# Ternary stage's weights, magnitudes, threshold, first ternary part and first two rows moved into the rotated attention's last batch

## The chip, the cores and the metric

One core of one Trainium2 chip. The metric is the device time of one execution in microseconds, the median of several runs. TensorE multiplies, VectorE, ScalarE and GpSimd compute elementwise and by rows, SyncE issues the transfers.

## The reference

A sequence of four layers, each an attention and a feed-forward part, all added to the residual x of 2048 rows by 512 (four sequences of 512). The change touches layer 2:

```python
x = x + _L2_attn_ref(_layernorm(x, axis=-1), q_w, q_b, kv_w, kv_b, o_w)
x = x + _L2_ffn_ref(_layernorm(x, axis=-1), w_fc, w_proj)

def _L2_attn_ref(x, q_w, q_b, kv_w, kv_b, o_w):
...
    q = _rope((x @ q_w.T + q_b) * scale)
    k = _rope(k)
    attn = jax.nn.softmax(jnp.einsum('bse,bte->bst', q, k), axis=-1)
    return jnp.einsum('bst,bte->bse', attn, v) @ o_w.T

def ternarize_weights(w):
    gamma = jnp.mean(jnp.abs(w))
    return jnp.sign(jnp.round(w / (gamma + EPS))) * gamma
def bitlinear(x, w):
    xn = layer_norm(x)
    x_hat = xn + jax.lax.stop_gradient(absmax_quant(xn) - xn)
    w_hat = w + jax.lax.stop_gradient(ternarize_weights(w) - w)
    return jnp.einsum('bsd,od->bso', x_hat, w_hat)
```

`_L2_ffn_ref` is bitlinear with w_fc, gelu, bitlinear with w_proj. A ternary weight can only be made once the mean magnitude of its whole matrix (w_fc or w_proj, 4 MB each) is known.

## The kernel before, in words

P = 128 partitions, D = 512, DC = 4 chunks of D, NB = 4 batches of TT = 4 tiles of 128 rows, NT = 16 tiles ("rows" below: row 0 is tile 0). The residual x stays in SBUF as 16 tiles. `build` calls one function for each stage; each stage is one `nc.Block`, in which every engine has its own program, and the next block starts when all engines have ended this one. Within a block the engines wait for one another by semaphores. An engine executes in order: whatever stands behind a waiting instruction waits too. `Jobs` gives each use of one of the eight PSUM banks a number, from which the waits for a bank being full, read or vacant follow. `product` (L99 to L103) makes one product out of three matmuls on high and low parts (fp32r pairs); `pair` reserves the high and low parts.

**attention512** ("a2", L1341). `ORDER` (L1390) is the order of the jobs by hand, and all five engines but SyncE walk through it. A batch is: four turns of the normalised rows ("T"), eight projections of q and k ("qk"), four of U = x times the folded value and output weights ("U"), then for each tile of 128 rows the scores ("S"), the transposes of the softmax ("PT") and the product with U ("PV"). ScalarE copies a PSUM bank to the high part, VectorE subtracts it to make the low part (`a_PT_lo` L1616, `a_U_lo` L1600). VectorE takes the negated row maximum (L1608), ScalarE the exponential with its sum (L1523), VectorE adds PV to x (L1627). GpSimd multiplies by the cosine (L1456), adds the bias to x (L1462), and for the rest of its time executes pieces of the "table" work (L335 to L345), which makes weights for the last stage; `table_moves` (L306) is the SyncE part of it: it fetches indices and stores finished parts, in order, with a wait for the table's steps. Batch 3 also takes the statistics of tiles 0 to 11 for the next stage (`tiles_ahead`, L490 and L495), four tiles behind each of the maxima of S 0, 1 and 2.

**ternary_feed_forward** ("f2", L1700). SyncE fetches `raw_fc` and `raw_pj` in four parts of 1 MB each. ScalarE sums the magnitudes of fc (L1788), VectorE those of pj (L1902). TensorE sums over the partitions (`total_of`, L1981), VectorE makes the threshold (`threshold`, L1873 to L1879). A ternary part is `(w > threshold) - (w < -threshold)`: the lower half into `below` by ScalarE (Sign L1803 and Relu L1805; five of the eight parts) or VectorE (L1895; three parts), then L1898 on VectorE. The statistics of the last four tiles come first (L209), GpSimd takes the roots of all 16 rows at once (`roots`, L253 to L262), VectorE normalises and clips a row (`row`, L1856 to L1863), TensorE turns it (L1975), ScalarE and VectorE split it (L1795, L1868).

For each tile t the loop then holds: the inner product F (32 matmuls on `fc`, L1991), gelu (L1812), statistics of the hidden row (`spread`, L1907 and L1911), GpSimd's root (L1773 to L1780), centring by ScalarE (L1816), the clip by VectorE (`clipped`, L1916 to L1920), 16 transposes (`turn_hidden`, L2001; the last four use a bank that is used by the first four, so they wait for L1925), the split (L1823, L1925), the outer product Y (32 matmuls on `pj`, L2012), and the add to x (L1930). TensorE's order is: turn(t+2), inner(t+1), outer(t-1), turn_hidden(t).

VectorE's order at the start sets much of what follows:

```python
prog.statistics(dve); row(0); row(1); turned_rest(0); turned_rest(1); row(2)
threshold(0); for n in range(4): ternary("fc", n)
magnitudes(0); magnitudes(1); spread(0); magnitudes(2); magnitudes(3)
threshold(1); clipped(0); turned_rest(2); row(3); spread(1); hidden_rest(0)
for n in range(4): ternary("pj", n)
```

Of the kernel before, what the change touches and what calls it, by code (L numbers as in the profile page):

```python
# [305 lines left out]
def table_moves(prog, sp, first, last):  # L306
# [179 lines left out]
def tiles_ahead(prog, dve, tiles):  # L486
# [7 lines left out]
    for t in tiles:  # L494
        dve.bn_aggr(prog.mv[:, t, :], prog.stats[:, t, :])  # L495
# [845 lines left out]
def attention512(prog, name, share):  # L1341
# [40 lines left out]
    rec = prog.sb(name + "_rec", [P, TT], F32)  # L1382

# [6 lines left out]
    for b in range(NB):  # L1390
# [13 lines left out]
        if b + 1 < NB:  # L1404
            ORDER += [("qk", b + 1, i) for i in range(len(QK))]

    BANK = {"T": lambda k: T_BANK[k], "qk": lambda k: k % 2, "vo": lambda k: 2 + k % 2, "const": lambda k: 4, "U": lambda k: 2 + k % 2,
            "S": lambda k: 4 + k % 2, "PT": lambda k: 6, "PV": lambda k: PV_BANK[k]}
# [16 lines left out]
    with nc.Block() as block:  # L1425
        @block.sync
        def _(sp):
# [5 lines left out]
            table_moves(prog, sp, *share)  # L1433

        @block.gpsimd
        def _(pool):
# [11 lines left out]
            for kind, b, k in ORDER:  # L1448
# [8 lines left out]
                elif kind == "U" and k == 0:  # L1457
# [5 lines left out]
                    if b + 1 < NB:  # L1463
                        roots(b + 1)

        @block.scalar
        def _(act):
# [4 lines left out]
            def finish(n):  # L1472
                hi, lo, whole = rope(n)
                act.wait_ge(*c_turn(0, n + 1))
                act.activation(hi, whole, ACT.Copy).then_inc(c_qkhi.sem, 1)

# [3 lines left out]
            for kind, b, k in ORDER:  # L1480
# [31 lines left out]
                elif kind == "U":  # L1512
                    act.wait_ge(*full(*key))
                    act.activation(U[0][:, k, :], bank(*key)[:, :], ACT.Copy).then_inc(c_uhi.sem, 1)
                elif kind == "S":
# [5 lines left out]
                    if b:  # L1521
                        act.wait_ge(*c_rec(0, t - TT + 1))
                    act.activation(Pr[t % 2][:, :], bank(*key)[:, :], ACT.Exp, bias=nm[:, k:k + 1],  # L1523
                                   accum_out=rs[:, k:k + 1]).then_inc(J.frees(key), 1)
                elif kind == "PT":
                    act.wait_ge(*full(*key))
                    act.activation(PT[0][:, :, k * P:(k + 1) * P], bank(*key)[:, :].rearrange("p (c n) -> p c n", c=TT), ACT.Copy).then_inc(c_pthi.sem, 1)

        @block.vector
        def _(dve):  # L1530
# [29 lines left out]
            for kind, b, k in ORDER:  # L1560
# [37 lines left out]
                elif kind == "U":  # L1598
                    dve.wait_ge(*c_uhi(0, b * TT + k + 1))
                    dve.tensor_tensor(U[1][:, k, :], bank(*key)[:, :], U[0][:, k, :].bitcast(F32), ALU.subtract).then_inc(J.frees(key), 1)  # L1600
                    if k == 1 and b + 1 < NB:
                        statistics(b + 1)
                elif kind == "S":
# [7 lines left out]
                    if k < 3 and b + 1 == NB:  # L1611
                        tiles_ahead(prog, dve, range(k * TT, (k + 1) * TT))
                elif kind == "PT":
# [7 lines left out]
                    dve.reciprocal(rec[:, k:k + 1], rs[:, k:k + 1]).then_inc(c_rec.sem, 1)  # L1621
                elif kind == "PV":
# [5 lines left out]
                                             ALU.mult, ALU.add).then_inc(J.frees(key), 1)  # L1628

        @block.tensor  # L1630
        def _(pe):
            for kind, b, k in ORDER:
# [41 lines left out]
                elif kind == "PT":  # L1674
                    pe.wait_ge(*read("S", b, k))
                    pe.wait_ge(*vacant(*key))
                    for c in range(TT):
                        last = pe.transpose(bank(*key)[:, c * P:(c + 1) * P], Pr[(b * TT + k) % 2][:, c * P:(c + 1) * P], prog.ident[:, :])
                else:
# [1695 lines left out]
```

## Time and profile before

| | us |
|---|---|
| median of 3 runs (3378.66, 3379.23, 3381.58) | 3379.23 |
| the profiled execution: span from its first to its last instruction | 3376.4 |
| the profiled execution's own time | not told apart from the three |
| TensorE busy | 2992.2 (89%) |
| VectorE busy | 1996.1 (59%) |
| ScalarE busy | 1551.2 (46%) |
| GpSimd busy | 1019.2 (30%) |
| mean granted TensorE clock | 0.936 |

The page gives busy time by engine and by groups of instructions; the views of the trace give single instructions in order of time with what ended the idle time before them. Times count from the first instruction. In the rows PE is TensorE's matmul, DVE is VectorE, ACT ScalarE, POOL GpSimd; a row merges neighbours of the same kind (x4). A granted clock of 1.00 is 2.4 GHz and one of 0.50 is 1.2 GHz; a stretch's figure is a mean.

### The profile page before, as it was taken

How to read it: one execution, taken by the hardware profiler on the slowest of the kernel's cores; microseconds unless marked ns; L12 is line 12 of the kernel's file. 1: busy time of each engine (PE TensorE's matmuls, PEld its weight loads, DVE VectorE, ACT ScalarE, POOL GpSimd, SP SyncE). 2: the span in 40 equal slices, each digit the busy share in tenths (PEclk: the TensorE clock that was granted, in tenths of full speed). 3: DMA queues.
4: the chain of work that ended last, by engine and by line, in shares of the span. 5: the costliest groups of instructions: out<-in, count | busy, mean ns of one | idle time of the engine just before them, and what ended most of it. 6: DMA issues, size and time to landing. Idle time of an engine off the chain costs nothing. (4 is left out here: it accounts for less than half of the span.)

```text
span 3376.4 us, 46857 instructions
## 1 busy us (share of the span) xinstructions
PE 2992.2 (89%) x16388; PEld 2260.9 (67%) x16388; DVE 1996.1 (59%) x5348; ACT 1551.2 (46%) x3598; POOL 1019.2 (30%) x1143
## 2 busy tenths in 40 slices
PE   6999799997999977978788767998689999989999
PEld 4777678885666645446566646775467777768887
DVE  5666587775555554233747767664678777742121
ACT  5777566664666652133222244444455555531000
POOL 3655333222444530000156640000133233322222
PEclk9999899998999987988899988999799999999999
DMA  2000301101000021203100020003100000020000
GB/s 87 2 2 1 113 32 32 32 32 63 1 2 1 2 67 64 100 7 117 66 4 4 2 101 1 1 1 119 34 1 1 1 1 1 1 103 13 13 13 13
DMA packets 65872, 105.51 MB, mean 31 GB/s; under 512 B 9315, under 2 KB 29795, under 8 KB 65509
## 3 DMA queue, kind: packets, MB, share of 16 engines
q1 hardware_dynamic: 65222, 102.41, 8.7%
q8 instruction: 132, 2.16, 0.3%
q14 instruction: 102, 0.84, 0.1%
q0 software_dynamic: 416, 0.10, 0.0%
HBM read 89.75 MB, written 12.85 MB: 30 GB/s over the span
## 5 line engine op out<-in xcount | busy, mean ns | idle before, releaser
L714 POOL TENSOR_SCALAR a_P<-a_P,a_rec 128x512 f32<-128x512 f32 (+3 forms) x256 | 301.5, 1190 | 350.9 <-DVE a_rec L872 350.9
L402 ACT ACTIVATE tree_value<-tree_bit,table_lut,tree_step 128x256 f32<-128x256 uint8 x496 | 275.3, 595 | 140.8 <-DVE tree_value L416 73.0
L416 DVE COPY_PREDICATED tree_value<-tree_bit,tree_value 128x256 f32<-128x256 uint8 x434 | 235.0, 547 | 133.3 <-ACT tree_value L402 104.9
L787 ACT ACTIVATE a_P<-a_P,a_low 128x384 f32<-128x384 f32 (+3 forms) x512 | 281.7, 558 | 25.0 <-DVE a_low L866 24.9
L101 PE MATMUL bank<-f_xT_hi,f_w_hi 128*128 128x512 f32 (+1 forms) x704 | 276.6, 393 | 14.0 <-DVE f_w_lo L1214 14.0
L102 PE MATMUL bank<-f_xT_hi,f_w_lo 128*128 128x512 f32 (+1 forms) x704 | 276.1, 392 | 0.0
L103 PE MATMUL bank<-f_xT_lo,f_w_hi 128*128 128x512 f32 (+1 forms) x704 | 275.7, 392 | 0.0
L1136 POOL CAST f_h_hi<-f_sg 128x512 fp32r<-128x512 f32 (+1 forms) x88 | 84.5, 961 | 587.6 <-DVE f_sg L1236 297.8
L866 DVE CUSTOM_DVE_ANT_0 a_P<-bank,a_causal 128x384 f32<-128x384 f32 (+3 forms) x512 | 222.9, 482 | 63.1 <-PE bank L949 62.6
L794 ACT ACTIVATE a_PT<-bank 128x512 f32<-128x512 f32 x320 | 174.2, 594 | 83.3 <-PE bank L960 82.6
L1236 DVE TENSOR_TENSOR f_sg<-bank,f_sg 128x512 f32<-128x512 f32 (+1 forms) x44 | 30.4, 691 | 269.4 <-PE bank L103 269.4
L960 PE MATMUL bank<-ident,a_P 128*128 128x128 f32 x1280 | 181.2, 287 | 9.2 <-issue 6.0
L960 PEld LDWEIGHTS bank<-ident,a_P 128*128 128x128 f32 x1280 | 148.9, 146 | 40.6 <-issue 30.0
L2342 ACT ACTIVATE a_PT<-bank 128x512 f32<-128x512 f32 x112 | 61.7, 595 | 220.6 <-PE bank L2615 220.6
L1172 ACT ACTIVATE f_sg<-bank 128x512 f32<-128x512 f32 (+1 forms) x44 | 26.3, 598 | 296.3 <-PE bank L103 296.2
L101 PEld LDWEIGHTS bank<-f_xT_hi,f_w_hi 128*128 128x128 f32 (+1 forms) x704 | 132.8, 189 | 43.3 <-issue 14.4
L102 PEld LDWEIGHTS bank<-f_xT_hi,f_w_lo 128*128 128x128 f32 (+1 forms) x704 | 132.8, 189 | 28.9
L103 PEld LDWEIGHTS bank<-f_xT_lo,f_w_hi 128*128 128x128 f32 (+1 forms) x704 | 132.6, 188 | 28.9
L101 PE MATMUL bank<-f_w_hi,f_h_hi 128*128 128x512 f32 (+1 forms) x352 | 140.9, 400 | 10.2 <-POOL f_h_lo L1138 10.2
L2329 ACT ACTIVATE a_P<-bank,a_nm,a_qs 128x256 f32<-128x256 f32 (+1 forms) x256 | 134.6, 545 | 22.1 <-DVE a_nm L2479 21.9
L102 PE MATMUL bank<-f_w_hi,f_h_lo 128*128 128x512 f32 (+1 forms) x352 | 138.7, 394 | 0.0
L103 PE MATMUL bank<-f_w_lo,f_h_hi 128*128 128x512 f32 (+1 forms) x352 | 138.6, 394 | 0.0
(464 smaller groups left out, 7922.7 us busy)
## 6 DMA issues: line engine op xcount, KB each, us to landing
f_w_raw<-in_f_w SPq DMA_DIRECT2D x11, 768.0 KB, 12.8
f_w_raw<-table_w SPq DMA_DIRECT2D x11, 768.0 KB, 11.2
tree_idx<-in_f_idx SPq DMA_DIRECT2D x62, 128.0 KB, 2.1
table_w<-tree_value SPq DMA_DIRECT2D x62, 128.0 KB, 1.7
x_res<-in_x SPq DMA_DIRECT2D x4, 1024.0 KB, 10.8
m_piece<-in_m_wq SPq DMA_DIRECT2D x2, 2048.0 KB, 12.1
m_piece<-in_m_wo SPq DMA_DIRECT2D x2, 2048.0 KB, 8.5
m_piece<-in_m_w_gate SPq DMA_DIRECT2D x2, 2048.0 KB, 10.4
```

Source lines behind the costliest of these rows:

```text
L101: pe.matmul(out, w[0], x[0], start=first, stop=False, skip_group_check=True)
L102: pe.matmul(out, w[1], x[0], start=False, stop=False, skip_group_check=True)
L103: return pe.matmul(out, w[0], x[1], start=False, stop=last, skip_group_check=True)
L402: act.activation(prog.tree_value[(h + to) % 4][:, :], prog.tree_bit[h % 2][0][:, :], ACT.Identity, bias=prog.table_lut[:, 2 * k:2 * k + 1] ...
L416: dve.copy_predicated(prog.tree_value[(h + keep) % 4][:, :], prog.tree_bit[h % 2][bit][:, :], prog.tree_value[(h + other) % 4][:, :]).then ...
L714: last = pool.tensor_scalar(Pr[j][:, g, col:col + n], Pr[j][:, g, col:col + n], rec[:, j, i, g:g + 1], None, ALU.mult)
L787: last = act.activation(Pr[j][:, k, col:col + n], Pr[j][:, k, col:col + n], ACT.Exp, bias=low[:, j, i, k:k + 1], scale=-1.0, accum_out=tot ...
L794: act.activation(PT[at % NPT][:, :], ps[J.bank(key)][:, :], ACT.Copy).then_inc(J.frees(key), 1)
L866: last = dve.tensor_tensor_reduce(out=Pr[j][:, k, col:col + n], in0=ps[J.bank(source)][:, col:col + n], in1=causal[:, T - n:T], scale=-sca ...
L960: last = pe.transpose(ps[J.bank(key)][:, g * P:(g + 1) * P], Pr[j][:, g, col + kt * P:col + (kt + 1) * P], prog.ident[:, :])
L1136: pool.tensor_copy(h[i % 2][0][0:n, :], sg[i % 2][0:n, :]).then_inc(c_hi.sem, 1)
L2329: e = act.activation(Pr[i][:, hh, lo:2 * P], ps[3 + j][:, h2 * 2 * P + lo:(h2 + 1) * 2 * P], ACT.Exp, bias=small["nm"][:, i, hh:hh + 1], s ...
```

## The change

The ternary stage's memory is laid out by a new function that `attention512` calls, on top of the attention's own: fc on the q and k weights, pj on the folded weights and xT, the scratch and lower halves on xn, U and QT, the rows on `flat`, the turned rows on `by_cos` and `by_sin`. In the attention's batch 3 each engine gets steps:

- SyncE, ahead of the store of the last table part: waits for the last qk product, fetches fc; waits for the last U, fetches pj.
- ScalarE: magnitudes of fc behind U 1, 2, 3 and S 0; copies of the two turned rows ("R"); lower half of fc part 1 at the end.
- GpSimd: roots of rows 0 to 3 behind the bias adds.
- VectorE: rows 0 and 1 behind U 1; their low parts ("R") behind the maximum of S 0; threshold 0 behind the maximum of S 3; lower half of fc part 0 behind PT 3, its ternary part behind PV 2. The statistics of tiles 0 to 3 go into batch 2, behind S 0.
- TensorE: two turns ("R") behind S 0, the sum behind S 2.

In the ternary stage ScalarE sums the magnitudes of pj too, the pj parts are made in the order 2, 3, 0, 1, with two of them ahead of the first clip, and the roots there are of rows 4 to 15.

```diff
@@ table_moves
     for i in range(first, last):
+        if i == last - 1:
+            before_last()
         sp.wait_ge(*prog.table_step(0, (i + 1) * TABLE_STEPS))
@@ attention512
+    for key, behind in ((("R", NB - 1, 0), ("S", NB - 1, 0)), (("R", NB - 1, 1), ("R", NB - 1, 0)), (("sum", NB - 1, 0), ("S", NB - 1, 2))):
+        ORDER.insert(ORDER.index(behind) + 1, key)
@@ sync
+            def next_weights():
+                sp.wait_ge(*full("qk", NB - 1, NQK - 1))
+                ternary_fetch(prog, sp, head, "f2", "fc")
+                sp.wait_ge(*full("U", NB - 1, TT - 1))
+                ternary_fetch(prog, sp, head, "f2", "pj")
@@ gpsimd
                     if b + 1 < NB:
                         roots(b + 1)
+                    else:
+                        roots_twice(prog, pool, slice(0, TT), 0)
@@ scalar
+                    if b + 1 == NB and k:
+                        magnitudes(k - 1)
+                elif kind == "R":
+                    act.wait_ge(*full(*key))
+                    act.activation(head.xT[k][0][:, :, :], bank(*key)[:, :].rearrange("p (c n) -> p c n", c=DC), ACT.Copy).then_inc(c_xhi.sem, 1)
...
+                    if t == NT - TT:
+                        magnitudes(3)
...
+                    if b * TT + k == NT - 1:
+                        ternary_beneath(prog, act, head, 0, 4)
@@ vector
+                    elif k == 1:
+                        dve.wait_ge(*prog.count("ln_rstd")(0, 1))
+                        ternary_row(prog, dve, head, 0)
+                        ternary_row(prog, dve, head, 1)
+                elif kind == "R":
+                    dve.wait_ge(*c_xhi(0, NT + k + 1))
+                    dve.tensor_tensor(head.xT[k][1][:, :, :], ..., ALU.subtract).then_inc(J.frees(key), 1)
...
-                    if k < 3 and b + 1 == NB:
+                    if k == 0 and b + 2 == NB:
+                        tiles_ahead(prog, dve, range(0, TT)).then_inc(prog.count("ln_mv").sem, 1)
+                    if 1 <= k < 3 and b + 1 == NB:
                         tiles_ahead(prog, dve, range(k * TT, (k + 1) * TT))
+                    if k == 3 and b + 1 == NB:
+                        dve.wait_ge(*full("sum", b, 0))
+                        ternary_threshold(prog, dve, head, 0, bank("sum", b, 0), 4 * D * D).then_inc(prog.count("w_gamma").sem, 1)
...
+                    if t == NT - 1:
+                        ternary_beneath_own(prog, dve, head, 1, "fc", 0)
...
+                    if t == NT - 2:
+                        ternary_make(prog, dve, head, "fc", 0)
@@ ternary_feed_forward, scalar
-            magnitudes(0)
-            magnitudes(1)
-            turned(0)
-            turned(1)
-            magnitudes(2)
-            magnitudes(3)
-            for i in range(3):
-                beneath(i)
-            gelu(0)
+            ternary_beneath(prog, act, M, 1, 0)
+            ternary_beneath(prog, act, M, 2, 0)
+            magnitudes(0)
+            magnitudes(1)
+            gelu(0)
+            magnitudes(2)
+            magnitudes(3)
@@ ternary_feed_forward, vector
-            prog.statistics(dve)
-            row(0)
...
-            magnitudes(3)
-            threshold(1)
+            ternary("fc", 1)
+            statistics()
+            ternary("fc", 2)
+            ternary("fc", 3)
+            row(2)
+            spread(0)
+            threshold()
+            ternary("pj", 2)
+            ternary("pj", 3)
             clipped(0)
             turned_rest(2)
             row(3)
             spread(1)
             hidden_rest(0)
-            for n in range(4):
-                ternary("pj", n)
+            ternary("pj", 0)
+            ternary("pj", 1)
@@ ternary_feed_forward, tensor
+                    if t == 1 and n == 3:
+                        total_of(1, c_psum)
...
-            turn(0)
-            turn(1)
-            total_of(0, c_fsum)
             inner(0)
```

In the functions called here, `magnitudes` is one Abs activation of 128 by 2048 with its sum, `ternary_row` the four instructions of `row`, `ternary_threshold` those of `threshold`, `ternary_beneath` the Sign and the Relu, `ternary_beneath_own` L1895, `ternary_make` L1898, `roots_twice` the seven steps of `roots` on part of the rows.

## Rows read from the trace of the kernel before

**Rows 1.** Busy time by stretch: stretch, us, engines, granted clock, DMA share, GB/s.
```profile
1975.50:2084.44 108.94, 63.14 (x261) 49.96 (x261) 79.23 (x102) 55.49 (x55) 11.97 (x23) 0.78 0.21 77
2084.44:2302.42 217.98, 210.41 (x1009) 169.26 (x1010) 144.59 (x217) 91.18 (x120) 15.80 (x50) 1.00 0.00 1
```

**Rows 2.** Timeline, TensorE: start, us, engine, line, what, [idle before, releaser].
```profile
1975.11 0.39 PE L103 MATMUL bank<-a_U_lo,a_PT_hi 128*128 128x512 f32 x1
...
2002.62 0.77 PE L1991 MATMUL bank<-f_fc,f_xT_hi 128*128 128x512 f32 x1 [4.57 <-issue]
...
2064.24 1.11 PE L2001 MATMUL bank<-ident,f_h 128*128 128x128 f32 x4 [8.76 <-DVE f_hT_lo L1925]
...
2084.44 0.66 PE L2001 MATMUL bank<-ident,f_h 128*128 128x128 f32 x4 [0.60 <-DVE f_hT_lo L1925]
...
2102.61 0.66 PE L2001 MATMUL bank<-ident,f_h 128*128 128x128 f32 x4 [0.60 <-DVE f_hT_lo L1925]
```

**Rows 3.** Timeline, VectorE, first part of the ternary stage.
```profile
1976.61 2.47 DVE L209 BATCH_NORM_STATS2 stats<-x_res 128x6 f32<-128x512 f32 x4 [0.32 <-PEq L1425]
...
1987.17 0.55 DVE L1856 TENSOR_SCALAR f_xn<-x_res,mv,rstd 128x512 f32<-128x512 f32 x1 [7.68 <-POOL rstd L262]
...
2012.77 4.47 DVE L1902 TENSOR_REDUCE f_sums<-f_raw_pj 128x1 f32<-128x2048 f32 x2
...
2025.76 2.29 DVE L1916 TENSOR_REDUCE f_hmax<-f_h 128x1 f32<-128x2048 f32 x1 [0.20 <-ACT f_h L1816]
...
2037.94 4.61 DVE L1898 SCALAR_TENSOR_TENSOR f_pj<-f_raw_pj,f_gamma,f_below 128x2048 fp32r<-128x2048 f32 x2
...
2049.88 2.28 DVE L1916 TENSOR_REDUCE f_hmax<-f_h 128x1 f32<-128x2048 f32 x1
```

**Rows 4.** Timeline, ScalarE, first part of the ternary stage.
```profile
1981.93 1.91 ACT L1788 ACTIVATE f_h<-f_raw_fc 128x2048 f32<-128x2048 f32 x1 [11.29 <-DMA f_raw_fc<-in_f_fc]
...
1998.85 2.00 ACT L1803 ACTIVATE f_below<-f_raw_fc,f_gamma 128x2048 f32<-128x2048 f32 x1 [1.44 <-DVE f_gamma L1879]
...
2010.48 1.28 ACT L1812 ACT_TABLE_LOAD   x1
...
2060.88 2.09 ACT L1816 ACTIVATE f_h<-f_h,f_hshift,f_hrstd 128x2048 f32<-128x2048 f32 x1 [14.69 <-POOL f_hshift L1780]
```

**Rows 5.** Timeline, GpSimd, batch 2, end of batch 3, ternary stage.
```profile
1873.97 1.04 POOL L1442 TENSOR_TENSOR rstd<-var,mhalf 128x4 f32<-128x4 f32 x1
...
1970.37 1.55 POOL L345 TENSOR_TENSOR table_sum<-table_sum,table_term 128x256 f32<-128x256 f32 x2
...
1979.94 2.94 POOL L257 TENSOR_TENSOR var<-var,mhalf 128x16 f32<-128x16 f32 x1
```

**Rows 6.** DMA issues of 1500 to 2000: KB each, median us to landing.
```profile
f_raw_fc<-in_f_fc SPq DMA_DIRECT2D x4, 1024.0 KB, 8.7
```

**Rows 7.** Busy time in one stretch of the first feed-forward stage.
```profile
400.00:420.00 20.00, 18.99 (x84) 15.40 (x83) 14.66 (x26) 14.29 (x22) 6.68 (x4) 1.00 0.60 219
```

**Rows 8.** Timeline of the attention's batches 2 and 3, several engines.
```profile
1880.74 0.69 DVE L1608 TENSOR_REDUCE a_nm<-bank 128x1 f32<-128x512 f32 x1 [1.40 <-PE bank L103]
...
1887.35 1.40 POOL L340 TENSOR_SCALAR table_term<-table_idx,table_lut 128x256 f32<-128x256 int32 x1
...
1932.99 1.74 DVE L1589 TENSOR_TENSOR a_KT_raw<-a_by_cos,a_by_sin 128x512 f32<-128x512 f32 x1
...
1952.68 0.69 DVE L1608 TENSOR_REDUCE a_nm<-bank 128x1 f32<-128x512 f32 x1 [1.40 <-PE bank L103]
...
1956.09 0.66 DVE L1608 TENSOR_REDUCE a_nm<-bank 128x1 f32<-128x512 f32 x1
...
1960.26 0.63 PE L1678 MATMUL bank<-ident,a_P 128*128 128x128 f32 x4 [1.69 <-DVE a_PT_lo L1616]
...
1968.42 0.69 DVE L1616 TENSOR_TENSOR a_PT_lo<-bank,a_PT_hi 128x512 fp32r<-128x512 f32 x1 [1.33 <-ACT a_PT_hi L1527]
...
1972.82 0.75 DVE L1627 SCALAR_TENSOR_TENSOR x_res<-bank,a_rec,x_res 128x512 f32<-128x512 f32 x1 [1.38 <-PE bank L103]
```

More of the change, by code:

```diff
@@ new lines, in ternary_fetch, with roots_twice, link @@
+def ternary_fetch(prog, sp, M, name, which):
+    raw, part, first = (M.raw_fc, M.fc_part, 0) if which == "fc" else (M.raw_pj, M.pj_part, 4)
+    for n in range(4):
+        source = part(prog.ins[f"{name}_{which}"].rearrange("(c p) n -> p c n", p=P), n)
+        sp.dma_start(part(raw, n), source).then_inc(prog.count(f"w_in{first + n}").sem, 16)
+def roots_twice(prog, pool, tiles, done):
+    c_mv, c_v, c_rstd = prog.count("ln_mv"), prog.count("ln_var"), prog.count("ln_rstd")
+    steps = 6 * done
+    def link(instruction):
+        nonlocal steps
+        steps += 1
+        instruction.then_inc(c_v.sem, 1)
+        pool.wait_ge(*c_v(0, steps))
+    var, n = prog.var, tiles.stop - tiles.start
+    pool.wait_ge(*c_mv(0, done + 1))
+    link(pool.tensor_scalar(var[:, 0, tiles], prog.mv[:, tiles, 1], 1e-5, None, ALU.add))
+    link(pool.tensor_tensor(var[:, 1, tiles], var[:, 0, tiles], prog.mhalf[:, 0:n], ALU.pow))
+    link(pool.tensor_tensor(var[:, 2, tiles], var[:, 1, tiles], var[:, 1, tiles], ALU.mult))
+    link(pool.tensor_tensor(var[:, 2, tiles], var[:, 2, tiles], prog.mv[:, tiles, 1], ALU.mult))
+    link(pool.tensor_scalar(var[:, 2, tiles], var[:, 2, tiles], 1e-6, None, ALU.add))
+    pool.tensor_tensor(var[:, 2, tiles], var[:, 2, tiles], prog.mhalf[:, 0:n], ALU.pow).then_inc(c_v.sem, 1)
+    pool.wait_ge(*c_v(0, steps + 1))
+    pool.tensor_tensor(prog.rstd[:, tiles], var[:, 1, tiles], var[:, 2, tiles], ALU.mult).then_inc(c_rstd.sem, 1)
@@ L1678, in _ @@
                         last = pe.transpose(bank(*key)[:, c * P:(c + 1) * P], Pr[(b * TT + k) % 2][:, c * P:(c + 1) * P], prog.ident[:, :])
+                elif kind == "R":
+                    pe.wait_ge(*prog.count("xn_ready")(0, k + 1))
+                    pe.wait_ge(*vacant(*key))
+                    for c in range(DC):
+                        last = pe.transpose(bank(*key)[:, c * P:(c + 1) * P], head.xn[k][:, c * P:(c + 1) * P], prog.ident[:, :])
+                elif kind == "sum":
+                    pe.wait_ge(*prog.count("w_sums")(0, 4))
+                    pe.wait_ge(*vacant(*key))
+                    last = pe.matmul(bank(*key)[:, 0:4], prog.ones[:, :], head.sums[:, 0:4], start=True, stop=True)
                 else:
@@ L1740, in ternary_feed_forward @@
     H_BANK = (4, 5, 6, 4)
[L1741 removed]
+    jobs = [(("F", 0, n), n) for n in range(4)]
     for t in range(NT):
@@ L1900, in magnitudes @@
-            def magnitudes(n):
-                dve.wait_ge(*w_in[4 + n](0, 16))
-                dve.tensor_reduce(sums[:, 4 + n:5 + n], pj_part(raw_pj, n), AX.XY, ALU.add, apply_absolute_value=True).then_inc(c_psum.sem, 1)
+                if (which, n) in BELOW_BY_DVE:
+                    own += 1
+                    ternary_beneath_own(prog, dve, M, own, which, n)
+                ternary_make(prog, dve, M, which, n)
             def spread(t):
```

247 lines of the change are left out of this document (146 added, 101 removed).

## The prediction

> **What bounds the kernel now.** I read the page first, where TensorE is by far the busiest engine, then busy time by stretch, the waits, and last the timeline engine by engine around the border of the two stages. A change elsewhere pays only where TensorE stands still. From the end of the attention's last product (1975.5) to 2084.44 TensorE is busy 63.1 of 108.9 us at a granted clock of 0.78; from there on it is busy 210.4 of 218 us at 1.00 [rows 1]. What the change can win lies in the first stretch; the second is TensorE's own and stays. Its period is seen at the last four transposes of a hidden row: 2084.44, 2102.61, so 18.17 us a row, with 0.60 us of waiting [rows 2].
>
> In the first stretch the engines wait for one another. The statistics of rows start at 1976.61, GpSimd's two powers take 2.94 us each, and row 0 starts at 1987.17 [rows 3, 5]. ScalarE waits 11.29 us for the first weights before it sums magnitudes [rows 4]; threshold 0 and fc part 0 follow, and the first ternary product starts at 2002.62, 27.1 us after the attention's last [rows 2]. Then VectorE is the bound. Its queue in order is the fc parts, two pairs of magnitude sums (the first takes 4.47 us), threshold 1, the clip of row 0 (from 2025.76), row 3, the statistics of row 1, the rest of the hidden row, and four pj parts (from 2037.94); the clip of row 1 begins only at 2049.88 [rows 3]. TensorE's last long wait, 8.76 us, comes of that, and it is on its period after 2084.44 [rows 2].
>
> **The change, part by part.** I follow one chain through. All clock times are those of the trace, with the new ones worked out from them. My anchor is the last four transposes of hidden row 2 (2084.44), since all later rows repeat the period.
>
> *Weights.* SyncE now asks for fc when TensorE has finished batch 3's last K product (about 1926.7) and for pj after its last U (1949.9). Before, the first part reached ScalarE 5.6 us behind the border: ScalarE's wait goes. An fc part took 8.7 us in the median to land [rows 6], the first about 5; part 3 is there by about 1940. The first magnitude is read at 1942.5. I cost the transfer at nothing; the cover is over 5 us for part 0 and over 14 for part 3, and beyond that every late us holds ScalarE. SyncE's queue: the wait stands ahead of the store of the last table part alone, whose last steps run at 1970.37 [rows 5]; the fetches of the table are all issued by then. Transfers ran beside dense TensorE work at 219 GB/s with the clock at 1.00 [rows 7], so TensorE gets no price for them.
>
> *Batch 2.* The statistics of rows 0 to 3 move there, behind the maximum of its first score tile (1880.74). In batch 3 the same work makes it 3.41 us from one maximum to the next (1952.68 to 1956.09) [rows 8]. The second maximum is then at 1884.15 instead of 1883.46, ScalarE's exponential and PT_lo follow 0.7 later, and TensorE's transposes, at 1886.48 now, at about 1887.0. TensorE is dense from there, so **+0.53**.
>
> *Batch 3, ScalarE.* Four magnitudes of 1.91 + 0.19 us [rows 4]. Three lie behind U 1 to 3, whose products take 2.7 us or more each; the fourth lies behind the first exponential, and two copies of the turned rows behind that. It ends about 1956.25, the copies at 1956.85 and 1957.35. No table load: Abs ran behind Exp without one.
>
> *Batch 3, GpSimd.* The power over 4 rows took 1.04 us against 2.94 over 16 [rows 5], so the old chain of 7.54 (1979.6 to 1987.14) becomes 3.76. It stands ahead of the table steps, which shift by it and by the 0.53: their end at 1976.2, the store's landing 2 us later.
>
> *Batch 3, VectorE.* Rows 0 and 1 (1.96 us each) come after U 1's rest, which ends at about 1943; the roots are ready at the same time, and the next U is due at 1947.9. Hidden. Then the queue in order costs: the rest of turned row 0 waits for ScalarE's copy (1956.85), two rests of 0.69 follow, and the second maximum starts at 1958.2 instead of 1956.09: **+2.1**. It carries the statistics and PT_lo behind it as now, so that TensorE's transposes, which even now wait 1.69 us there [rows 8], start at 1962.35 instead of 1960.26. The turns of the two rows and the sum (about 1.1 us of TensorE) lie in that longer wait. From 1960.26 to the end TensorE is dense now, so its end is 2.1 later. Threshold 0 (0.78 us) lies in the 1.33 us that VectorE waits before PT_lo; the lower half of fc part 0 (1.29) in the 1.38 before an add [rows 8]; its 2.35 us stand ahead of the last add, which starts 0.35 late: **+0.35**. ScalarE makes the lower half of fc part 1 (3.9 us from 1972.8) before the border. Sum for the border: 1976.61 + 0.53 + 2.1 + 0.35 = 1979.6.
>
> *One place where two engines meet in SBUF.* While GpSimd adds the bias to the residual rows, VectorE's add of 0.68 us takes 1.74; while VectorE normalises four rows, GpSimd's step of 1.15 us takes 1.40 [rows 8]. In the new order VectorE's four row operations, the 1.29 and the 2.35 lie beside table steps. Bounds: nothing, and one step of 1.15 for each of the three groups, 3.5 us. I take **+0.4**, near the normalising row, since most of it falls into waits. The Trainium skill ("SBUF — State Buffer", Who interferes with whom) says that VectorE in a two-port mode or with two SBUF inputs and GpSimd exclude each other for a whole instruction; taken at its word each of six operations could wait for a step, some 7 us, and the trace speaks for less. New border: **1980.0**, 3.4 later.
>
> *Behind the border, ScalarE sets the first part.* Two lower halves 2 x 3.85 (2.00 and 1.91, slightly overlapped), pj magnitudes 0 and 1 2 x 2.05, table load 1.30, gelu 0 2.5, magnitudes 2 and 3 2 x 2.05 [rows 4]: 19.7, so 1999.7. Sum and threshold 1, 0.45 and 0.79: 2000.9. VectorE is done with fc 1 to 3, row 2 and the statistics of hidden row 0 at about 1996.8, and TensorE with the inner products up to the third of row 1 at 1999.5, so both just wait. Pj 2 and 3 with their own lower halves, 7.4 us (2042.55 to 2049.88 now) [rows 3]: 2008.3. The clip of row 0 starts there instead of 2025.76, takes 3.86: 2012.2. From its end to the rest of the hidden row 8.32 as now (2029.62 to 2037.94): 2020.5. Pj 0 and 1 are then only 4.61 [rows 3]: 2025.1. The clip of row 1 starts there, 24.8 us before today's 2049.88. What it releases: clip 3.85, row 4 and the turn's rest 2.46, statistics 2.87, GpSimd 1.8: ScalarE centres row 2 at 2036.1 instead of 2060.88 [rows 4], and the last four transposes of row 1 come 3.36 later: 2039.5 instead of 2064.24. TensorE's own way there ends at 2037.1 even as slow as now, so it waits 2.4 us instead of 8.76. From those transposes to the next took 20.20 us now, after a wait that left TensorE on the lower clock; after waits of 1.69 and 1.71 it kept the upper one. I take 18.17: 2057.7.
>
> **Sum:** 2084.44 - 2057.7 = 26.7 us less. The profiled span is 3376.4 us and the median of three runs 3379.23, so 2.8 us lie around the span; which run was profiled the page does not say. 3379.2 - 26.7 = 3352.5.
>
> **Unknown prices.** (a) TensorE's clock in the first two inner products: it has only four groups of 1.85 us in 12 us. If it falls, ten products at 0.43 instead of 0.23 (as from 2002.62) cost 2.0 and push threshold 1 by 1.7; with the last period at 20.20 that makes 3.7. I take nothing, the lower end. (b) Magnitudes 2 and 3 run behind Gelu. The trace has Copy, Identity, Sign and Relu behind its load without another, but not Abs. Bounds: nothing and two loads of 1.28 [rows 4], 2.6. I take nothing, as for the four neighbours. The Trainium skill ("ScalarE: Activation LUTs", Table sets) has abs in every set, which is the lower bound; were it not so, the sum would be 24.1.
>
> **Rivals.**
> *One or two of these prices are paid*: the clock of (a), the loads of (b), the table store holding the border. Gain 21 to 25: 3354.5 to 3358. For it: GpSimd's 1976.2 plus 2 us stands only some 1.5 us before the border. 0.20.
> *Attention takes more*: the queues in order in batch 3 hold back further links (U 3's copy behind a magnitude, row 0 behind the roots). For it: GpSimd and VectorE are already late there, as the 1.74 shows. Each missed link costs 2 to 4 us, two or three of them 5 to 12: 3358 to 3365. 0.10.
> *More is won*: some of the 3.4 us at the border vanishes because the copies do not hold the maximum, and the last wait of 2.4 too. Gain 28 to 31: 3348 to 3351. 0.12.
> *It does not do what it says*: fc is early, yet TensorE meets the clip of row 0 where it does now, since the pj work sets it. Gain under 6.8. Against it: two magnitude pairs leave VectorE [rows 3]. 0.03.
> *Slower*: the weights come too slowly beside the attention. Magnitude 3 is read at 1954.7; a late part holds the copies, the maximum and TensorE, us for us. To eat 26.7 us fc must land after 1981, 4.19 MB in 52 us, so below 80 GB/s from 1929 on. Beside busy TensorE 219 GB/s were seen [rows 7]. 0.02.
> Forecast: 0.53.
>
> **Range and chances.** 3348.5 to 3361 leaves out half of the second rival, all of the last two and the tip of the best case. A difference of 0.2% is 6.8 us, about what a measurement here can tell from no change. Faster by more: forecast and the first three rivals, 0.95; same 0.03; slower 0.02.
>
> **What would show it.** Right: the first ternary product within 1 us of the border; border near 1980; the second maximum of batch 3 about 2 us later and TensorE's wait there 2.8 us; threshold 1 near 20 us behind the border; clip of row 1 near 45 us behind it instead of 73; one wait of 2 to 3 us before the period of 18.17, which stays. Wrong: a wait of ScalarE for f_raw_fc, a table load at the pj magnitudes, TensorE's low clock in batch 3, or the border set by the table store.

## The result, and the profile after

The changed kernel takes 3343.16 us (median of 4 runs, 3339.56 to 3348.12), the kernel before beside it 3378.94 (4 runs): a ratio of 0.9894, 95% interval 0.9883 to 0.9906. Run twice more below, it gave 0.9910 and 0.9903. The mean of the three ratios, 0.9902, is 33 us less; 26.7 were predicted, and 3343.16 lies 5.3 below the range. The profiled execution of after took 3348.12 us, with a span of 3346.3: 30.1 less than before's 3376.4.

Busy time by stretch answers to [rows 1] (stretch, us, engines with their instructions, granted clock, DMA share, GB/s): from 1975.50, where the attention's last product ended before, to the prediction's anchor, and from there to the stage's end.

```profile
1975.50:2058.33 82.83, 61.46 (x269) 49.60 (x267) 65.49 (x87) 53.68 (x53) 15.01 (x25) 0.88 0.01 2
2058.33:2288.78 230.45, 222.27 (x1088) 183.11 (x1088) 152.71 (x226) 93.97 (x125) 15.75 (x50) 1.00 0.00 1
```

The kernel before, from its anchor to the end of the stage:

```profile
2084.44:2319.93 235.49, 227.31 (x1088) 182.60 (x1088) 152.78 (x226) 93.95 (x125) 15.80 (x50) 1.00 0.00 1
```

TensorE reaches the anchor with 21.4 us of idle time (82.83 less 61.46) where [rows 1] have 45.8. The second stretch I had forecast as unchanged: the same 1088 matmuls at the same granted clock take 230.45 us instead of 235.49, so 5.0 less. TensorE's timeline (start, us, engine, line, what, idle before and releaser) has both effects:

```profile
1943.52 0.79 PE L101 MATMUL bank<-a_wvo_hi,a_xT_hi 128*128 128x512 f32 x1 [10.21 <-DVE a_U_lo L1769]
...
1962.93 0.63 PE L1866 MATMUL bank<-ident,a_P 128*128 128x128 f32 x4 [2.41 <-DVE a_PT_lo L1800]
...
1964.14 0.63 PE L101 MATMUL bank<-a_U_hi,a_PT_hi 128*128 128x512 f32 x1
...
1979.39 0.39 PE L103 MATMUL bank<-a_U_lo,a_PT_hi 128*128 128x512 f32 x1
1981.31 0.47 PE L2135 MATMUL bank<-f_fc,f_xT_hi 128*128 128x512 f32 x1 [1.52 <-PEq L1570]
...
2013.41 2.82 PE L2145 MATMUL bank<-ident,f_h 128*128 128x128 f32 x12 [10.04 <-DVE f_h L2067]
...
2040.56 0.66 PE L2145 MATMUL bank<-ident,f_h 128*128 128x128 f32 x4 [3.03 <-DVE f_hT_lo L2072]
...
2058.33 0.66 PE L2145 MATMUL bank<-ident,f_h 128*128 128x128 f32 x4 [0.60 <-DVE f_hT_lo L2072]
...
2076.09 0.66 PE L2145 MATMUL bank<-ident,f_h 128*128 128x128 f32 x4 [0.60 <-DVE f_hT_lo L2072]
```

The first ternary product starts 1.5 us after the attention's last ends (27.1 before [rows 2]); the wait of 8.76 us has become 3.03; and from 2058.33 to 2076.09 a row takes 17.76 us instead of 18.17.

The profile counts from the program's start, and unchanged code ahead of the stage moves by some us between executions: U 0 of batch 3 (the first of that batch's U products, the first line above) starts at 1942.39 before and 1943.52 here, and between 1938.9 and 1947.3 in runs below. So I compare stretches that begin at that product. Before, it is 142.05 us to the anchor; here 114.81 (114.83 and 114.89 in the two further profiles): 27.2 less. Batch 2 gives 0.5 back, so **26.7** is gone by the anchor. That equals the predicted sum, although two of its steps came out otherwise and cancelled (below). The rest comes behind the anchor: 5.0 to the stage's end. Against it, the next stage's wait for its own weights is 11.06 instead of 10.18, and this execution was 0.6 late before anything changed (U 0 of batch 2 at 1870.82 instead of 1870.22). Together 30.2, of which the spans show 30.1. Those last two terms are not the change's: in the two further profiles the next stage's wait is 10.11 and 10.39.

VectorE's timeline at the links that the prediction names:

```profile
1953.62 0.69 DVE L1785 TENSOR_REDUCE a_nm<-bank 128x1 f32<-128x512 f32 x1 [1.40 <-PE bank L103]
1957.54 1.29 DVE L1778 TENSOR_TENSOR f_xT_lo<-bank,f_xT_hi 128x512 fp32r<-128x512 f32 x2 [3.23 <-ACT f_xT_hi L1679]
1958.74 0.68 DVE L1785 TENSOR_REDUCE a_nm<-bank 128x1 f32<-128x512 f32 x1
...
1981.15 2.35 DVE L1449 SCALAR_TENSOR_TENSOR f_fc<-f_raw_fc,f_gamma,f_below 128x2048 fp32r<-128x2048 f32 x1 [0.32 <-PEq L1570]
...
2001.46 0.16 DVE L1407 TENSOR_REDUCE f_gamma<-bank 128x1 f32<-128x4 f32 x1 [3.63 <-PE bank L2122]
...
2009.51 2.28 DVE L2063 TENSOR_REDUCE f_hmax<-f_h 128x1 f32<-128x2048 f32 x1
...
2026.20 2.27 DVE L2063 TENSOR_REDUCE f_hmax<-f_h 128x1 f32<-128x2048 f32 x1
```

The 3.23 us is the predicted hold-up: VectorE stands at the turned rows until ScalarE has copied them, and the second maximum waits behind it. From the border (1981.15) threshold 1 is 20.3 us away, the clip of row 0 28.4, the clip of row 1 45.1; predicted were 20.1 (2000.9 less the 0.79 of the threshold itself), 28.3 and 45.1.

ScalarE runs its magnitudes behind Gelu with one table load, and it no longer waits for weights at all:

```profile
1992.93 1.28 ACT L1975 ACT_TABLE_LOAD   x1
1994.23 2.42 ACT L1975 ACTIVATE f_h<-bank,f_gamma 128x512 f32<-128x512 f32 x4
1996.53 1.93 ACT L1962 ACTIVATE f_scrap<-f_raw_pj 128x2048 f32<-128x2048 f32 x1
```

### The profile page after: what moved, and what is told of

Read it like the earlier page. It is cut to its first block and busy times, and to the rows that moved or that the text cites. A ratio compares the mean times of both kernels' runs of the same rounds, so it can differ in the third digit from the quotient of the medians.

```text
span 3346.3 us, 46876 instructions
## 1 busy us (share of the span) xinstructions
PE 2981.3 (89%) x16388; PEld 2258.7 (67%) x16388; DVE 1985.8 (59%) x5344; ACT 1558.3 (47%) x3606; POOL 1024.1 (31%) x1150
```

## The experiments

Two questions stood open: where the 5 us behind the anchor come from, and whether the chain that I followed is the one that holds the time (so that loosening or loading a link moves the anchor as the chain says).

**The changed kernel again**, for the noise of one comparison.

> The changed kernel once more, to learn how far its 3343 us (four runs, 3339.6 to 3348.1) is the kernel and how far the run. Its trace accounts for 30.1 us: 26.1 at the last four transposes of hidden row 2, 5.4 in the thirteen rows behind (period 17.76 instead of 18.17 us), -1.4 elsewhere. If that is all, the ratio is 0.9911 (30 us); if the runs hold more than one execution shows, it stays near 0.989 (36 us).

3345.93 us (6 runs) against 3379.29 (17): 0.9910, 0.9895 to 0.9924. The stretch from U 0 to the anchor was 114.83, the period (from one row's last transposes to the next row's) 17.76 to 17.79. Both differences belong to the kernel and not to one execution.

Six of the versions below ran once each: before_hT 3378.15 us, after_hT64 3347.26, before_up64 3372.84, before_steps 3374.32, after_R_behind_PV 3350.68, after_mag_on_dve 3351.84. Runs of one kernel lie some 10 us apart, so for these the trace decides and not the time.

**Places in SBUF.** The change moves the stage's tensors. The edit gives the kernel before the new relative places, and nothing else: the two small tiles go behind hT, so everything between them starts 64 bytes lower.

```diff
-    gamma = prog.sb(name + "_gamma", [P, 8], F32)
-    sums = prog.sb(name + "_sums", [P, 8], F32)
     below = ...
...
     hT, _ = prog.pair(name + "_hT", [P, NI, P])
+    gamma = prog.sb(name + "_gamma", [P, 8], F32)
+    sums = prog.sb(name + "_sums", [P, 8], F32)
```

> The kernel before, with only the two small tiles gamma and sums laid behind hT, so that below, xT, xn, h and hT lie 64 bytes lower, in step with fc and pj modulo 2048 bytes as in the changed kernel. Theory 'place': TensorE's pace depends on how the addresses of the stationary and the moving operand stand to each other; the period falls from 18.17 to about 17.76 and the time by some 6 us (16 rows). Rival 'traffic': the pace comes of what the other engines do in the changed kernel; the period stays 18.17 and the time the same.

3372.79 us (12 runs) against 3379.29 (17): 0.9984, 0.9976 to 0.9992, 5.4 us by the ratio. The same view in groups, 2110 to 2250 (line, operation, shape, count, busy us, mean ns of one, idle), the kernel before:

```profile
L2012 PE MATMUL bank<-f_pj,f_hT_lo 128*128 128x512 f32 x128 | 50.6, 395 | 0.0
L1991 PE MATMUL bank<-f_fc,f_xT_lo 128*128 128x512 f32 x117 | 46.2, 395 | 0.0
```

and with the places moved:

```profile
L2012 PE MATMUL bank<-f_pj,f_hT_lo 128*128 128x512 f32 x128 | 49.8, 389 | 0.0
L1991 PE MATMUL bank<-f_fc,f_xT_lo 128*128 128x512 f32 x124 | 48.3, 390 | 0.0
```

These durations overlap in the pipeline; the distance from start to start is what counts. 32 inner products take 7.38 us instead of 7.55, 32 outer ones 7.26 instead of 7.47: both quicker, at the same granted clock of 1.00. The period is the changed kernel's:

```profile
2086.59 0.66 PE L2001 MATMUL bank<-ident,f_h 128*128 128x128 f32 x4 [0.60 <-DVE f_hT_lo L1925]
2104.38 0.66 PE L2001 MATMUL bank<-ident,f_h 128*128 128x128 f32 x4 [0.60 <-DVE f_hT_lo L1925]
```

From its anchor to the stage's end it takes 230.45 us (2086.59 to 2317.04), to the hundredth as in the changed kernel. So the 5.0 us are no part of the reordering. Ahead of the anchor the new places are worth little by themselves: U 0 to the anchor is 141.75 instead of 142.05.

**Only one of the two operands in step.** The addresses, worked out from the two programs: the weights fc and pj lie at 704 bytes modulo 2048 in both kernels; before, xT and hT lie at 768, after at 704. "In step" below means this, the same place modulo 2048 as the weights. First only hT is moved, in the kernel before:

```diff
+    prog.at += 1984
     hT, _ = prog.pair(name + "_hT", [P, NI, P])
```

> The kernel before with hT alone moved by 1984 bytes, so that hT is in step with pj and xT stays out of step with fc. Place: the outer product's 32 matmuls take 7.27 us instead of 7.47 from their start to the next group's, the inner product's stay at 7.55 instead of 7.38. Traffic: both stay.

Outer products became quick (7.27 to 7.29 per 32), inner ones stayed slow (7.55); the period is 17.98, half of the gain.

**The reverse in the changed kernel**: the same line with `+= 64`.

> The changed kernel with hT 64 bytes higher, out of step with pj; xT stays in step. Place: outer back to 7.47 us, inner stays at 7.38, period 17.96, time +3 us. Traffic: outer stays at 7.27, period 17.76.

Inner 7.38, outer 7.47, period 17.99. Each loop follows its own pair of tensors, and 64 bytes suffice to lose it.

**Own place or distance?** The kernel before with the small tiles last, the stage's weights 64 bytes higher (so that xT is in step with them), and hT 128 bytes off pj:

```diff
-    prog.at = prog.stage_at
+    prog.at = prog.stage_at + 64
...
+    prog.at += 128
     hT, _ = prog.pair(name + "_hT", [P, NI, P])
```

> Of the kernel before with the small tiles last: fc and pj, below, xT, xn and h 64 bytes up (xT again in step with fc, but each at a multiple of 128 bytes now), and hT 192 bytes up, 128 bytes off pj's place modulo 2048. 'Relation': the pace depends on the distance between the two operands; the inner product takes 7.38 us as in the kernel in step. 'Alignment': it depends on the stationary operand's own address modulo 128; the inner product takes 7.55 and the outer 7.47. If relation holds, the outer product tells its period: 7.27 if 128 bytes (or a part of it), 7.47 if more.

Inner products are quick (7.40). xT lies at the very address that it has in the kernel before, where they are slow (7.55); only fc has moved. So the distance decides and not xT's own place. Outer ones are slow (7.44): 128 bytes off is not in step either.

**Which distances?** Small tiles last, so all in step, then xT 32 bytes further and hT 1024:

```diff
+    prog.at += 32
     xT = ...
...
+    prog.at += 1024 - 32
     hT, _ = prog.pair(name + "_hT", [P, NI, P])
```

> The kernel before with the small tiles last (all in step), then xT 32 bytes up and hT 1024 bytes up. If the pace asks for equal places modulo 2048, both products go at the slow pace (7.55 and 7.47 us). If it asks only for equal places modulo 1024 or less, the outer goes at 7.27; 128 bytes off was slow. If 32 bytes are near enough, the inner goes at 7.38.

Inner 7.54: 32 bytes off is slow. Outer 7.26: 1024 off is quick.

```profile
L2014 PE MATMUL bank<-f_pj,f_hT_lo 128*128 128x512 f32 x128 | 49.8, 389 | 0.0
L1993 PE MATMUL bank<-f_fc,f_xT_lo 128*128 128x512 f32 x121 | 47.8, 395 | 0.0
```

The programs narrow it further. From one 128-row chunk to the next, the tile of xT or hT moves on by 512 bytes and that of fc or pj by a multiple of 2048, so the distance modulo 1024 alternates between two values 512 apart. No chunk is slower for it: with all in step (before_phase), outer products start 0.227 to 0.229 us apart at each of the four chunk places, and out of step (the kernel before) 0.233 to 0.235. So 512 bytes off is quick too. What matters is the distance between the two operands modulo some size above 128 and at most 512 bytes. Which size, and what in the chip makes it so, stays open.

**One term loaded: the pj magnitudes back on VectorE** (in the changed kernel, two pairs as before).

```diff
-            magnitudes(0)
-            magnitudes(1)
             gelu(0)
-            magnitudes(2)
-            magnitudes(3)
...
             row(2)
+            magnitudes(0)
+            magnitudes(1)
             spread(0)
+            magnitudes(2)
+            magnitudes(3)
             threshold()
```

> The changed kernel with the four magnitude sums of pj back on VectorE (between row 2 and the statistics of hidden row 0, and behind them), as before the change. Theory: VectorE's queue then has 8.9 us more and threshold 1 comes about 3.9 us later against the border, so does the clip of row 0, and the last four transposes of row 2. Rival (threshold 1 is set by TensorE's inner products, which stand ahead of the sum): no difference, within 1 us.

VectorE's timeline, and TensorE's with the anchor:

```profile
1978.36 2.35 DVE L1449 SCALAR_TENSOR_TENSOR f_fc<-f_raw_fc,f_gamma,f_below 128x2048 fp32r<-128x2048 f32 x1 [0.32 <-PEq L1570]
...
1990.38 4.47 DVE L2043 TENSOR_REDUCE f_sums<-f_raw_pj 128x1 f32<-128x2048 f32 x2
...
2010.64 2.28 DVE L2057 TENSOR_REDUCE f_hmax<-f_h 128x1 f32<-128x2048 f32 x1
```

```profile
2061.05 0.66 PE L2143 MATMUL bank<-ident,f_h 128*128 128x128 f32 x4 [0.60 <-DVE f_hT_lo L2066]
```

The clip of row 0 is 32.3 us behind the border instead of 28.4 (+3.9), the anchor 82.7 instead of 77.2 (+5.5). The 1.6 between them comes from TensorE's lower clock level: the two groups of 32 inner products ahead of the anchor took, from the first start to the last end, 9.38 and 9.13 us instead of 8.06 and 7.52, 2.9 more, of which the last wait gives 1.3 back (1.70 instead of 3.03). The chain sets the time, with the clock as an addition.

**One wait taken out: the row turns behind PV 0.** The transposes of rows 0 and 1 (R) leave the place ahead of the second maximum.

```diff
-(("R", NB - 1, 0), ("S", NB - 1, 0))
+(("R", NB - 1, 0), ("PV", NB - 1, 0))
```

> The changed kernel with only the two R jobs moved behind PV 0 of batch 3. Theory (VectorE's queue in order held the second maximum until ScalarE had copied the turned rows, 2.1 us): the second maximum comes 3.4 us behind the first again or sooner, TensorE waits there under 1.7 us instead of 2.41, and the last product of the attention ends 1.0 to 1.5 us earlier than in the changed kernel. Rival (the wait is set by the statistics of four rows and not by the copies): the attention's end stays or moves later by the 0.75 us of the turns.

The attention's end came earlier, as expected, and the border did not follow:

```profile
1942.85 0.79 PE L101 MATMUL bank<-a_wvo_hi,a_xT_hi 128*128 128x512 f32 x1 [10.24 <-DVE a_U_lo L1769]
...
1959.86 0.63 PE L1866 MATMUL bank<-ident,a_P 128*128 128x128 f32 x4 [0.92 <-DVE a_PT_lo L1800]
...
1981.42 0.76 PE L2135 MATMUL bank<-f_fc,f_xT_hi 128*128 128x512 f32 x1 [5.39 <-PEq L1570]
```

TensorE's wait fell from 2.41 to 0.92 us, and the attention's last product ends 33.2 us behind U 0 instead of 36.3: 3.1 earlier where 1.0 to 1.5 were expected. The transposes start 2.4 earlier, the products behind the wait also keep the upper clock level (1.6 more, see "Batch 3" below), and the two row turns now stand among those products (0.8 back). Then it stands 5.39 us at the border, 38.6 behind U 0 instead of 37.8. GpSimd's last steps of the table say why:

```profile
1974.32 3.10 POOL L342 TENSOR_SCALAR table_term<-table_idx,table_lut 128x256 f32<-128x256 int32 x1
1977.51 1.52 POOL L347 TENSOR_TENSOR table_sum<-table_sum,table_term 128x256 f32<-128x256 f32 x2
```

A step that takes 1.14 us takes 3.10 beside VectorE's make of fc part 0 (L1449, 2.34 us from 1974.07), and the table's store, which every engine waits for at the border, leaves at 1979.1. The Trainium skill ("SBUF — State Buffer", Who interferes with whom) lets a VectorE operation with two SBUF inputs and a GpSimd one that reads SBUF exclude each other for a whole instruction; this row agrees, at 1.96 us. The wait has only changed its owner; in the changed kernel SyncE, done with the store, still waits 1.4 us for the others, so that much was to spare. The expectation had left the border out.

The anchor comes 116.9 us behind U 0, 2.1 later, though the clip of row 1 is only 0.4 late (83.1 instead of 82.7 behind U 0). The other 1.6 is TensorE's clock in the last inner product ahead of the anchor. The same group of 32 products in the changed kernel, and then here:

```profile
2041.64:2049.00 7.36, 7.36 (x35) 6.10 (x34) 7.00 (x11) 2.88 (x5) 0.00 (x0) 1.00 0.01 2
```

```profile
2041.41:2050.38 8.97, 8.97 (x35) 7.26 (x34) 8.61 (x13) 2.88 (x5) 0.00 (x0) 0.81 0.01 2
```

The granted clock of that group is 0.82 in the kernel before, 1.00 in all three profiles of the changed kernel, and 0.81 again with the magnitudes on VectorE. TensorE's wait just ahead of it does not explain the level: 3.03 us in the changed kernel, 1.65 here. What sets it was not tested.

**More of the work early** ("the early version" below): R behind PV 0, all four pj magnitudes in batch 3, TensorE's total of them at its first product and threshold 1 behind fc part 1, pj part 2 ahead of the statistics of hidden row 0.

```diff
+                    if b + 1 == NB and k == 0:
+                        magnitudes_pj(0)
+                    if b + 1 == NB and k == 1:
+                        magnitudes_pj(1)
+                        magnitudes_pj(2)
                     if b * TT + k == NT - 1:
+                        act.wait_ge(*prog.count("w_total")(0, 3))
                         ternary_beneath(prog, act, head, 0, 4)
+                        magnitudes_pj(3)
...
             ternary("fc", 1)
+            threshold()
             statistics()
...
-            spread(0)
-            threshold()
             ternary("pj", 2)
+            spread(0)
```

> The changed kernel with the two turned rows (R) behind PV 0 of batch 3 instead of behind S 0, and with the four magnitude sums of pj in batch 3 on ScalarE (one behind PT 0, two behind PT 1, one behind the lower half of fc part 1), threshold 1 behind fc part 1 and pj part 2 ahead of the statistics of hidden row 0. Theory (ScalarE's 8.2 us of magnitudes behind the border hold threshold 1 and with it VectorE's queue): clip of row 0 comes about 6 us earlier against the border, the border itself about 1.3 earlier; the last four transposes of row 2 about 6 to 7 us before today's 2058.3, the time 3338 to 3341 where the changed kernel has 3346. Rival (ScalarE's idle time in batch 3 is not free: its exponentials and copies then come late and TensorE waits): border 2 to 4 us later, time 3342 to 3346.

The gain did not come: 3347.19 us against 3383.46, 0.9893 (0.9873 to 0.9913), and the anchor is 114.83 us behind U 0, to 0.02 as in the changed kernel. Threshold 1 now comes at 1984.29, but GpSimd took over as the engine that is waited for, at the border and behind it:

```profile
1974.87 3.29 POOL L342 TENSOR_SCALAR table_term<-table_idx,table_lut 128x256 f32<-128x256 int32 x1
1978.24 1.52 POOL L347 TENSOR_TENSOR table_sum<-table_sum,table_term 128x256 f32<-128x256 f32 x2
1988.13 2.27 POOL L1473 TENSOR_SCALAR var<-mv 128x12 f32<-128x12 f32 x1 [8.37 <-DVE mv L2024]
1990.49 5.25 POOL L1474 TENSOR_TENSOR var<-var,mhalf 128x12 f32<-128x12 f32 x1
1995.81 2.33 POOL L1475 TENSOR_TENSOR var<-var 128x12 f32<-128x12 f32 x1
```

The roots of rows 4 to 15 took 5.25 us for a power that takes 2.30 alone, and 2.33 for a product of 0.25; VectorE's makes lie beside both. They stand ahead of the root of hidden row 0, so the clip of row 0 waits 3.93 us for ScalarE, and ScalarE for that root. Even so the clip of row 1 comes 81.4 us behind U 0 instead of 82.7; that 1.3 is lost again in the row that ends at the anchor, at the lower clock: its inner product takes 8.11 us instead of 7.36 at a granted clock of 0.90, and the transposes just before it 0.5 more.

**The same with GpSimd relieved** (the relieved version): eight table pieces run behind the vo jobs of batch 0, where GpSimd stood idle, and the roots of rows 4 to 15 run behind the root of hidden row 0.

```diff
-            table = TableShare(prog, share, 3 * NT)
+            table = TableShare(prog, share, 3 * NT + 2 * DC)
...
+                elif kind == "vo":
+                    pool.wait_ge(*full(kind, b, k))
+                    table.run(pool)
+                    table.run(pool)
...
-            roots_twice(prog, pool, slice(TT, NT), 1)
             for t in range(NT):
...
+                if t == 0:
+                    roots_twice(prog, pool, slice(TT, NT), 1)
```

> c1_pj_early with two further edits, both on GpSimd. (1) Eight more pieces of the table work behind the four vo jobs of batch 0, so that batch 3 has 26.6 steps of it instead of 31. (2) In the ternary stage the roots of rows 4 to 15 come behind the first hidden row's root instead of ahead of it. Theory: in c1 the border was held by the last table store (TensorE idle 5.3 us there), and the clip of row 0 by the roots, which VectorE's two-input operations had stretched to 16 us. Then the border comes 3 to 4 us earlier (TensorE waits 1.5 to 2.5 us there), the clip of row 0 about 3 us earlier against the border, the time 5 to 8 us under c1 and under the changed kernel. Rival: the table work in batch 0 holds the bias adds and with them batch 0's end; then no gain.

```profile
1941.66 0.80 PE L101 MATMUL bank<-a_wvo_hi,a_xT_hi 128*128 128x512 f32 x1 [10.21 <-DVE a_U_lo L1786]
...
1976.51 0.35 PE L2130 MATMUL bank<-f_sums,ones 128*128 128x4 f32 x2 [1.52 <-PEq L1570]
...
2005.96 2.82 PE L2151 MATMUL bank<-ident,f_h 128*128 128x128 f32 x12 [8.00 <-DVE f_h L2075]
...
2052.37 0.66 PE L2151 MATMUL bank<-ident,f_h 128*128 128x128 f32 x4 [0.60 <-DVE f_hT_lo L2080]
```

3343.27 us (4 runs) against 3381.22 (7): 0.9882, 0.9865 to 0.9898. The border is 34.9 us behind U 0 (the early version 38.8, the changed kernel 37.8), the anchor 110.7: 4.1 us ahead of the changed kernel, where 5 to 8 were expected. The clip of row 1 is 5.6 us ahead, and the same row takes 1.5 of it back (granted clock 0.86, 8.47 us for the inner product). GpSimd still costs something too: the power of hidden row 0's root takes 2.64 us instead of 0.58 beside VectorE's make of a pj part, and the clip of row 0 waits 3.31 us for ScalarE. In the same comparison the **changed kernel, a third time**, has 0.9903 (0.9889 to 0.9918); the two intervals overlap, so that the relieved version is the better one rests on the trace. It is the quickest kernel of the study by both.

> The changed kernel beside the one above on the same chip: ratio 0.989 to 0.991 as in its ten runs so far.

3348.64 us (4 runs), anchor 114.89 behind U 0, as twice before.

## Why the prediction was wrong, point by point

**Direction and mechanism were right up to the anchor.** The forecast case came by its own steps. That its sum was met to 0.1 us there is partly luck: the border came 0.5 us later than forecast, and the row before the anchor took 17.77 us instead of 18.17, 0.4 less, by the new pace that the forecast did not have.

- *Weights.* No wait of ScalarE for them in the profile after. SyncE issued fc and pj in time, and TensorE showed no price for the transfers.
- *Batch 2.* Forecast +0.53. The transposes there now wait 0.34 us, and from U 0 of batch 2 to U 0 of batch 3 it is 72.70 us instead of 72.17: +0.53.
- *Batch 3, the second maximum.* Forecast +2.1 for the attention's end; it became +3.15 (36.26 us from U 0 to the end, before 33.11). The queue in order gave less, 1.5 us: the transposes start 19.41 behind U 0, before 17.87. The other 1.6 is a price that I did not list there: behind the wait of 2.41 us (before 1.69) eight products of PV 0 run at the lower of the two clock levels, 0.43 us from start to start, so PV 0 takes 4.42 us where PV 1 takes 2.86. This was my "TensorE's low clock in batch 3", named only among the signs of being wrong. With a wait of 0.92 us in its place (R behind PV 0) the end comes at 33.2 again.
- *Meetings in SBUF.* Forecast +0.4 of up to 3.5. The border's own part, from the end of the last product to VectorE's first operation behind it, grew from 1.11 to 1.37 us, so by 0.3 against 0.35 + 0.4 forecast. That was luck as much as sizing: the make of fc part 0 started at 1977.83, 0.1 us behind the table's last step. In the two runs in which it lay beside table steps, single GpSimd steps grew by 2.0 and 2.2 us, and the border came 0.8 to 1.0 us later although the attention ended some 3 us earlier.
- *The border*: forecast 37.1 us behind U 0 (34.22 before, 2.1, 0.35 and 0.4), measured 37.63.
- *ScalarE's first part, threshold 1, both clips.* 20.3, 28.4 and 45.1 us behind the border, against 20.1, 28.3 and 45.1. The magnitudes' four turns on VectorE, 8.9 us by their rows, are worth 3.9 at the clip and 5.5 at the anchor (run with them back).
- *Unknown prices.* (a) The clock's two signs did not come: threshold 1 was not late, and from the last wait to the anchor it is 17.77 us, not 20.20. The second was luck: I took the upper level because short waits (1.69 and 1.71 us) had kept it. In the changed kernel it was kept after 3.03 us, and in four variants it was lost after 1.65 to 2.37 us, at 1.3 to 1.6 us each (19.07 to 19.38 for that row). (b) Abs behind Gelu needs no load. The Trainium skill ("ScalarE: Activation LUTs", Table sets) has abs in every set, and the trace agrees: one load, at 1992.93, and none beside the magnitude at 1996.53.
- *The last wait and the anchor.* Forecast 2.4 and 77.7 behind the border, measured 3.03 and 77.2.

**The step that failed** is "all later rows repeat the period", with the second stretch "TensorE's own" that "stays" and a period of 18.17. I took the pace of the matmuls as given by their shape and the clock. The change also lays out the stage's tensors anew, and that makes xT and hT lie in step with the weights: 17.76 us a row. That is the 5.0 us, and the run with the new places alone gained the same in the trace and 5.4 (2.7 to 8.1) by its ratio.

A smaller step is wrong too: the sum puts 2.8 us between the span and the time, but the records of all runs show 1.8 (3346.3 and 3348.12, for one), so the forecast starts 1.0 too high for the execution that was profiled. The profiled execution of the changed kernel took 3348.12 us, 4.4 less than forecast: 5.0 and 1.0, less the 0.9 and 0.6 of this one execution, to 0.1. The median of 3343.16 lies another 5 lower, so more than half of the 9.3 us between forecast and median is no step of the sum. The medians of the two later comparisons are 3345.93 and 3348.64, the last just inside the range: single comparisons scatter by that much (each interval is some 4 to 5 us to either side), and nothing in the trace asks for a further cause. None of my rivals held the new pace: "more is won" looked for its 28 to 31 us in waits at the border. A period that I had not allowed to move, and a range whose lower end left 4 us for everything beyond the sum, put the result outside.

**The rivals.** "One or two prices are paid" held in part (the low clock, but in batch 3), and was made up for by 0.6 of the queue, 0.5 at the border and 0.4 of the new pace. "Attention takes more" did not come in the changed kernel, but the early version shows how near it was: its expected gain went into the table's store, the roots on GpSimd and, for the last 1.3 us, the clock. "It does not do what it says" and "slower" are out by the first ternary product and by ScalarE's queue.

## What to carry to other kernels

A reordering that also changes the memory layout is two changes: compare the start-to-start distance of like matmuls before and after, and test the layout by itself. When a link is loosened, ask which engine is second at the same barrier; here it was GpSimd's table, with 1.4 us to spare, and of the three versions that did more work early or freed a queue only the one that relieved it too reached the anchor sooner. Follow a single chain from a product that both traces share, not from the trace's origin, which moved by up to 8 us between executions. When a predicted sum is met, check its terms too: here an error of 0.5 us and one of 0.4 cancelled.

## What the runs showed of the hardware

- At equal clock, fp32r matmuls of 128x512 go from one start to the next in 0.231 and 0.227 us (inner, outer) when stationary and moving operand lie the same number of bytes into SBUF modulo a size above 128 and at most 512, and in 0.236 and 0.233 when they are 32, 64 or 128 bytes off. That is 2.5%, and 0.2% of this kernel.
- A GpSimd operation beside a VectorE one with two SBUF inputs can take 2 to 3 us longer (1.14 to 3.10 and 3.29; 2.30 to 5.25).
- A wait of 2.41 us of TensorE in a dense stretch was followed by eight products at the lower clock level, the one of 0.92 us in its place by none. The length of the wait alone does not tell: ahead of the anchor, waits of 3.03, 1.65 and 1.70 us were followed by a granted clock of 1.00, 0.81 and 0.81.
- Runs of one kernel in one comparison spread over some 10 us (3374 to 3384 and 3377 to 3390 for the kernel before), and part of it is there before the changed part begins (three profiles of the changed kernel reach U 0 of batch 3 at 1941.96, 1943.52 and 1947.33).
